# Second attention of a fused graph network: turning x by DMA transposes of f16 halves instead of TensorE transposes

## The reference

```python
q = heads(features @ Wq); k = heads(features @ Wk); v = heads(features @ Wv)      # 8 heads of 32
e = jnp.einsum('whqd,whkd->whqk', q, k)
e = jnp.where(e >= 0, e, ALPHA * e)
attn = jax.nn.softmax(jnp.where(adj[:, None] > 0, e, NEG), axis=-1)
h = jnp.einsum('whqk,whkd->whqd', attn, v)
out = _layernorm(h, g1, b1)
out = jnp.concatenate([out, features], axis=-1) @ Wffn.T
out = _layernorm(out, g2, b2)
return out + features
```

## Time and profile before

| | |
|---|---|
| median of three runs | 3160.52 us (3158.16 to 3162.86) |
| profiled execution, its own time | 3157.04 us |
| its span, first to last instruction | 3155.3 us |
| TensorE busy | 3019.6 us, 96% of the span |
| VectorE, ScalarE, POOL busy | 2482.2, 1999.8, 1672.7 us |
| mean granted TensorE clock | 0.987 of 2.4 GHz |

### The profile page before, as it was taken

One profiled execution on the slowest core, in us unless ns is written; L12 is line 12 of the kernel. 1 busy time (PEld: TensorE's weight loads), 2 busy tenths in 40 slices (PEclk: granted clock), 3 DMA queues, 4 the chain that ended last, 5 costly groups with the idle time before them and its releaser, 6 DMA issues.

```text
span 3155.3 us, 75174 instructions
## 1 busy us (share of the span) xinstructions
PE 3019.6 (96%) x27909; PEld 2049.3 (65%) x27909; DVE 2482.2 (79%) x6757; ACT 1999.8 (63%) x3695; POOL 1672.7 (53%) x1511
## 2 busy tenths in 40 slices
PE   6999999999999976999999998999999999999996
PEld 4666666666666644666666676777777777777773
DVE  5888888888888864666666667888888888888883
ACT  4666656666666644666666656777777777777774
POOL 2555555555554542344444435666666666666665
PEclk9999999999999998999999999999999999999998
DMA  5444444544454423222222224444444444444441
GB/s 163 138 135 140 135 140 131 144 129 145 130 144 131 142 62 92 76 77 78 81 68 81 77 86 142 136 136 147 137 142 140 138 142 135 136 147 137 142 129 41
DMA packets 358327, 382.45 MB, mean 121 GB/s; under 512 B 99264, under 2 KB 266816, under 8 KB 357952
## 3 DMA queue, kind: packets, MB, share of 16 engines
q1 hardware_dynamic: 356800, 376.03, 40.3%
q10 hardware_dynamic: 1152, 1.52, 0.2%
HBM read 242.16 MB, written 118.49 MB: 114 GB/s over the span
## 4 chain that ended last, share of the span: by engine, by line
PE 54%; DVE 2%; DMA 2%; issue 1%; ACT 1%; SPq 1%; POOL 0%; POOLq 0%; DVEq 0%; ACTq 0%
PE bank_heads L2267 4%; PE bank_pair L2146 4%; PE bank_pair L2535 3%; PE bank_pair L2537 3%; PE bank_pair L2536 3%; PE bank_score L2171 3%; PE bank_pair L2149 3%; PE bank_pair L2160 3%; PE bank_proj L2131 2%; PE bank_proj L2133 2%; PE bank_proj L2132 2%; PE bank_back L2131 2%; PE bank_heads L2535 2%; PE bank_heads L2536 2%; PE bank_heads L2537 2%; PE bank_sums L2536 2%
## 5 line engine op out<-in xcount | busy, mean ns | idle before, releaser
L1865 ACT ACTIVATE f_gh<-bank_pair 128x512 f32<-128x512 f32 x512 | 304.3, 594 | 247.3 <-PE bank_pair L2149 247.2
L2488 DVE TENSOR_TENSOR f_gl<-f_act,f_gh 128x512 f16<-128x512 f32 x256 | 281.9, 1101 | 227.1 <-ACT f_act L2416 227.1
L2075 DVE CUSTOM_DVE_ANT_0 b_junk<-bank_score,b_mask 128x256 bf16<-128x256 f32 x1024 | 390.6, 419 | 42.1 <-issue 41.8
L1409 DVE TENSOR_TENSOR a_linked<-a_prob,a_mask 128x1024 f32<-128x1024 f32 x256 | 354.0, 1383 | 3.9 <-ACT a_prob L1206 3.9
L1968 POOL TENSOR_TENSOR f_xb<-f_gh 128x512 f32<-128x512 f32 x256 | 335.6, 1311 | 36.0 <-ACT f_gh L1865 35.7
L2411 ACT ACTIVATE f_gh<-bank_pair,s_f_b 128x512 f16<-128x512 f32 x256 | 175.7, 686 | 252.7 <-PE bank_pair L2537 252.6
L1952 POOL TENSOR_TENSOR b_nw_root<-b_nw_var,b_minus_halves 128x2 f32<-128x2 f32 x128 | 113.0, 883 | 406.8 <-DVE b_nw_neg_mean L2016 406.8
L1206 ACT ACTIVATE a_prob<-a_score_t 128x1024 f32<-128x1024 f32 x256 | 259.5, 1014 | 109.0 <-PE a_score_t L1489 103.0
L1402 DVE TENSOR_REDUCE a_neg_max<-a_score 128x4 f32<-128x1024 f32 x256 | 307.5, 1201 | 2.7 <-PE a_score L1502 2.6
L1871 ACT ACTIVATE bank_pair<-bank_pair 128x512 f32<-128x512 f32 x512 | 305.4, 596 | 0.0
L1447 DVE SCALAR_TENSOR_TENSOR a_qk<-a_proj,a_vcol,a_qk 128x256 f16<-128x256 f32 x256 | 112.1, 480 | 136.6 <-ACT a_qk L1217 136.6
(11 more groups left out here) (275 smaller groups left out, 9748.3 us busy)
## 6 DMA issues: line engine op xcount, KB each, us to landing
a_stack<-qk_scratch SPq DMA_DIRECT2D x384, 128.0 KB, 3.0
qk_scratch<-a_qk SPq DMA_DIRECT2D x64, 512.0 KB, 2.9
qk_scratch<-b_qk SPq DMA_DIRECT2D x64, 512.0 KB, 2.9
first_rows<-qk_scratch SPq DMA_DIRECT2D x192, 128.0 KB, 3.0
f_gl<-qk_scratch SPq DMA_DIRECT2D x192, 128.0 KB, 2.8
a_x_sb<-x_t SPq DMA_DIRECT2D x64, 256.0 KB, 3.3
a_adj_sb<-adj_t SPq DMA_DIRECT2D x64, 256.0 KB, 3.1
a_res<-x_nodes SPq DMA_DIRECT2D x64, 256.0 KB, 3.4
```

Of the source, the lines that this page charges most:

```text
L1409: nc.vector.tensor_tensor(linked[:, k], prob[:, k], mask[:, be[1] % 2].unsqueeze(1).to_broadcast([P, 2, NT * N]), ALU.mult).then_inc(link_ ...
L1865: nc.scalar.activation(prob[:, he], score_t[s].rearrange("p t n -> p (t n)"), ACT.Exp, scale=ALPHA).then_inc(exp_done, 1)
L2075: last = nc.vector.tensor_tensor_reduce(junk[:, s, it], score[s][:, it], mask[:, i, it], -1.0, 3e38, ALU.add, ALU.min, neg_max[:, i, col:c ...
L2488: nc.vector.tensor_tensor(gl[:, bu[1] % 2, f], act32[:, f % 2], gh[:, bu[1] % 2, f], ALU.subtract).then_inc(low_done, 1)
```

## The change

x comes in by nodes, is split by nodes, and the halves are turned by the DMA queue SP. A new buffer `x_nodes` holds both halves by nodes for two graphs. In `AT`, `load` moves from 4 to 0, `xh` from 8 to 6, `xl` from 9 to 7, and a new stage `turn_x` on SP is at 7: the load is issued in slot 0, and six slots later ScalarE splits, VectorE one slot after that. ScalarE's `xh` and VectorE's `xl` now read `x_sb` in SBUF, not the bank. TensorE's `xT` is gone, so bank `proj` is used by `q`, `k` and `v` alone.

```diff
-    AT = {"load": 4, "load_adj": 4, "xT": 8, "xh": 8, "xl": 9, "q": 10, ...
+    AT = {"load": 0, "load_adj": 4, "xh": 6, "xl": 7, "turn_x": 7, "q": 10, ...
+        x_nodes = sb("x_nodes", [P, 2, 2, DC, NT, P], F16)
...
                     if bx := due(t, h, "load"):
                         i = bx[1] % XS
-                        if (n := after(back(bx, XS), 4, 1)) is not None:
-                            sp.wait_ge(proj_done, n)
+                        if (n := after(back(bx, XS), 1, 1)) is not None:
+                            sp.wait_ge(xh_ready, n)
+                            sp.wait_ge(xl_ready, n)
                         sp.dma_start(x_sb[:, i], rows(x_in, bx)).then_inc(x_loaded[i], 16)
+                    if bx := due(t, h, "turn_x"):
+                        i, r = bx[1] % 2, bx[1]
+                        if number(bx) == EARLY:
+                            wait_old(sp, "up_done")
+                        if (n := after(back(bx, XB), 1, 1)) is not None:
+                            sp.wait_ge(out_done, n)
+                        for ready, half, k in ((xh_ready, xh, 0), (xl_ready, xl, 1)):
+                            sp.wait_ge(ready, count(bx, 1, 1))
+                            sp.dma_start_transpose(half[r].rearrange("p c n -> p (c n)").rearrange("p (g n) -> p g n", n=P),
+                                                   x_nodes[:, i, k].rearrange("p c t n -> p (c t n)")).then_inc(x_turned[i], 16)
...
                     if bx := due(t, h, "xh"):
-                        act.wait_ge(proj_done, count(bx, 4, 1))
-                        if number(bx) == EARLY:
-                            wait_old(act, "up_done")
-                        if (n := after(back(bx, XB), 1, 1)) is not None:
-                            act.wait_ge(out_done, n)
-                        nc.scalar.activation(xh[bx[1]], proj[:],
-                                             ACT.Copy).then_inc(xh_ready, 1)
+                        i = bx[1] % 2
+                        act.wait_ge(x_loaded[i], uses(bx, XS) * 16)
+                        if exists(back(bx, 2)):
+                            act.wait_ge(x_turned[i], uses(back(bx, 2), 2) * 32)
+                        nc.scalar.activation(x_nodes[:, i, 0].rearrange("p c t n -> p t c n"),
+                                             x_sb[:, i].rearrange("p t (c n) -> p t c n", c=DC), ACT.Copy).then_inc(xh_ready, 1)
...
                     if bx := due(t, h, "xl"):
-                        r = bx[1]
+                        i = bx[1] % 2
                         dve.wait_ge(xh_ready, count(bx, 1, 1))
-                        nc.vector.tensor_tensor(xl[r], proj[:].rearrange("p (c n) -> p c n", c=DC), xh[r], ALU.subtract).then_inc(xl_ready, 1)
+                        nc.vector.tensor_tensor(x_nodes[:, i, 1].rearrange("p c t n -> p t c n"),
+                                                x_sb[:, i].rearrange("p t (c n) -> p t c n", c=DC),
+                                                x_nodes[:, i, 0].rearrange("p c t n -> p t c n"), ALU.subtract).then_inc(xl_ready, 1)
...
-                    if bx := due(t, h, "xT"):
-                        pe.wait_ge(x_loaded[bx[1] % XS], uses(bx, XS) * 16)
-                        if number(bx) == 0:
-                            wait_old(pe, "row_out")
-                        if (n := after(back(bx, 1), 1, 1)) is not None:
-                            pe.wait_ge(v_ready, n)
-                        for c in range(DC):
-                            for tt in range(NT):
-                                last = nc.tensor.transpose(proj[:, c * N + tt * P:c * N + (tt + 1) * P],
-                                                           x_sb[:, bx[1] % XS, tt, c * P:(c + 1) * P], ident[:])
-                        last.then_inc(proj_done, 1)
                     for j, name in enumerate(("q", "k")):
                         if bp := due(t, h, name):
                             if j == 0:
-                                pe.wait_ge(xl_ready, count(bp, 1, 1))
+                                pe.wait_ge(x_turned[bp[1] % 2], uses(bp, 2) * 32)
+                                if number(bp) == 0:
+                                    wait_old(pe, "row_out")
+                                if (n := after(back(bp, 1), 1, 1)) is not None:
+                                    pe.wait_ge(v_ready, n)
```

More of the change, by code:

```diff
@@ L1613, in attention_second @@
     LATE = 3
-    AT = {"load": 4, "load_adj": 4, "xT": 8, "xh": 8, "xl": 9, "q": 10, "q_hi": 10, "q_lo": 11, "linked": 7, "k": 12, "k_hi": 12, "k_lo": 13,
+    AT = {"load": 0, "load_adj": 4, "xh": 6, "xl": 7, "turn_x": 7, "q": 10, "q_hi": 10, "q_lo": 11, "linked": 7, "k": 12, "k_hi": 12, "k_lo": 13,
           "count": 9, "any": 9, "v": 14, "v_out": 14, "zero_q": 12, "far": 10, "store_qk": 13, "mask": 15, "S": 17, "max": 17,
@@ L1731, in attention_second @@
         proj_done = sem("proj_done")
+        x_turned = [sem(f"x_turned{i}") for i in range(2)]
         xh_ready = sem("xh_ready")
@@ L1911, in slot @@
                             i = bp[1] % 2
-                            act.wait_ge(proj_done, count(bp, 4, j + 2))
+                            act.wait_ge(proj_done, count(bp, 3, j + 1))
                             if j == 0 and exists(back(bp, 2)):
@@ L1916, in slot @@
                     if bx := due(t, h, "xh"):
-                        act.wait_ge(proj_done, count(bx, 4, 1))
-                        if number(bx) == EARLY:
-                            wait_old(act, "up_done")
-                        if (n := after(back(bx, XB), 1, 1)) is not None:
-                            act.wait_ge(out_done, n)
-                        nc.scalar.activation(xh[bx[1]], proj[:],
-                                             ACT.Copy).then_inc(xh_ready, 1)
+                        i = bx[1] % 2
[4 more added lines that the diff above has]
+                                             x_sb[:, i].rearrange("p t (c n) -> p t c n", c=DC), ACT.Copy).then_inc(xh_ready, 1)
                     if bp := due(t, h, "v_out"):
-                        act.wait_ge(proj_done, count(bp, 4, 4))
+                        act.wait_ge(proj_done, count(bp, 3, 3))
                         if number(bp) == EARLY:
```

## The result

The kernel after takes 3167.62 us, the median of eight runs (3165.22 to 3171.74); the kernel before takes 3159.53 us over eight runs (3154.54 to 3162.86). The ratio is 1.0025, with a 95% interval of 1.0015 to 1.0036: 8 us slower. The forecast was 3162 us, range 3142 to 3190, and said that the likeliest was a change within 0.2%.

A forecast was written before the change was run, and what follows sets the result against it. TensorE was taken as the bound, with y on VectorE only 0.20 us from delaying turn_max. Terms +3.5 - 1.5 = +2 us on 3157.04 gave 3159, said as 3162 us for the median of runs; range 3142 to 3190.

The forecast's parts named there:

- `turn_max` and `y`: Slot 1: TensorE's 0.44 us is lost waiting for y; turn_max starts 0.06 us later, +3.5 us over 58 steps.
- The last link: From neg_some through offset and y to turn_max: y ends at 2545.60, turn_max starts 0.08 us later at 2545.68.
- rival 4: VectorE: xl hidden in its waits, y ends as now, turn_max 0.12 us earlier, 3152 us; chance 0.14.
- The first steps: Steps at the start that have no y: may give back up to 1 us more.
- DMA waits: S in slot 1, waiting for a stack in 16 graphs, may come 0.06 us later without cost: some 1 us back.
- Transposes: Two on SP, slot 7: issue 0.62 to 1.23 us each, land before q; cost 0, at most 0.15 us a graph.
- Rival 3: SP: transposes slow throughout, ending 3.4 us after q is due, 197 us over 58 steps, 3358 us; chance 0.02.
- `xh` and `load`: xh moved to slot 6 on ScalarE, hidden behind out_x products; load moved to slot 0; cost 0 for both.
- The sum: Whole kernel: +3.5 - 1.5 = +2 us on the profiled 3157.04 us, so 3159; as median of runs 3162.
- The likeliest case: Whole kernel: the forecast of 3162 us, own range 3154 to 3172, chance 0.50.
- the side that I had given 8 in 100: Whole kernel: the forecast's share of 0.08 for a time more than 0.2% slower.

The follow-up runs named there:

- xl_psum: Kernel after with xl reading a PSUM bank of scores instead of SBUF, comparing instead of subtracting; 3156.26 us, ratio 1.0006.
- xh_last: Kernel after with xh behind v_out on ScalarE, so that xl misses POOL's gap; 3221.65 us, ratio 1.0214.
- after_pad: Kernel after with 72 more already-satisfied waits on TensorE at the program's start; 3160.2 us, ratio 1.0018.
- before_pad: Kernel before with 218 more already-satisfied waits on TensorE at the program's start; 3169.2 us, ratio 1.0043.
- control pair: Both kernels unchanged, one further profile of each; 3156.97 us for the kernel before, 3164.28 us for the kernel after.
- plain_copy: Kernel after with each DMA transpose replaced by a plain DMA of the same bytes, x not turned; 3160.8 us, ratio 1.0024.
- control_after: Kernel after, unchanged, profiled a second time; 3164.28 us.
- xl_early: Kernel after with xh in slot 1, xl in slot 2 behind max, transposes in slot 4; 3180.0 us, ratio 1.0084.
- xl_early2: Kernel after with xh in slot 2, xl in slot 2 behind stats1, transposes in slot 4; 3181.21 us, ratio 1.0072.

## Why the prediction was right, and where its size was off

- **`turn_max` and `y`.** Right: TensorE's 0.44 us a graph is lost whole in a wait for `y`. Counted from the start of `turn_z`, the steps were forecast and measured as: end of `xl` 2.56 and 2.55 us, end of POOL's third affine 3.68 and 3.68, `linked` 3.97 and 3.97, `mask` 5.37 and 5.38, `neg_some` 6.52 and 6.54, `y` 7.42 and 7.35, start of `turn_max` 7.50 and 7.46. `xl_psum` and `xh_last` show the cause from both sides.
- **The last link.** `y` came 0.07 us earlier than forecast. In the kernel before it started at 2544.73, 0.01 us after `offset`, and I took that for its bound; but TensorE's `out` had ended at 2544.42 + 0.27 = 2544.69 (its last matmul), so `y` could have gone 0.04 us earlier at most. In the kernel after `out` ends 0.44 us earlier (2550.08 + 0.27 = 2550.35), and `y` starts 0.08 us before `offset` ends. So the step measured +0.033 us in place of +0.06: 1.8 us over 54 graphs where 3.5 stood in the sum for 58. The same bound makes rival 4 worth more than I gave it: with POOL not held `turn_max` starts at 7.25 us, 0.20 us earlier than before and not 0.12.
- **The first steps, "may give back up to 1 us more".** This is the term that failed. They cost 3.5 us in the profiled pair, and 6.0 to 7.4 us in five other profiles with the split in slots 6 and 7 (77.9 to 79.3 us against a mean of 71.9 for the two profiles of the kernel before). I had asked which waits there would shrink and not what the removed instructions move. The mechanism, in order: fewer TensorE instructions; an instruction packet inside the q/k store of graph 3; the store lands after 4.48 us instead of 2.92; `S`, counted from the start of the store, comes 1.8 us later (1936.20 - 1926.38 against 1932.79 - 1924.77); and 3.4 us more at the lower clock. `after_pad` and `before_pad` show it in both directions.
- **DMA waits, "1 us given back".** Wrong in sign. What goes beyond 54 undisturbed graphs is 6.0 and 5.3 us in the two profiles of the kernel after, 4.3 and 3.6 in those of the kernel before: +1.7 us. The landing of the stack's last block does not explain it: it comes 6.86 against 6.67 us after `turn_z` in the profiled pair (medians of 48 graphs), but 6.61 against 6.62 in the control pair, and 6.63 with plain copies, whose 54 graphs had 5.7 us beyond as well. The traces do show where these waits stand. In both kernels, their controls, the padded kernels and `plain_copy`, the 24 to 29 graphs without an instruction packet from 0.3 us ahead of the start of their q/k store to 8.5 us behind it lose 0.0 to 0.5 us together; the others lose the rest, 3.6 to 4.3 us with `xT` and 4.3 to 6.0 us with the split. Why a packet costs more with the split stays open.
- **Transposes.** That they hide was right: the weight loads of `q` waited for them three times in 64 graphs, 2.0 us in all. Their issue did not halve with their size: it takes 1.26 us, above my upper bound of 1.23. The second lands 8.0 us after `turn_z` instead of the 6.9 to 7.6 forecast, 1.36 us ahead of `q`. Rival 3 fell: the Trainium skill, page "VectorE: DVE Perf Modes", section "The three transpose paths", gives 1309 ns for a 128x128 bf16 tile by DMA, an estimate from that page of 5.2 us for the four tiles of one transpose. The trace does not agree with that product: here four tiles landed 2.9 us after the issue.
- **`xh` and `load`.** Cost 0, as forecast: slots 6 and 7 take 2.633 and 3.292 us in both kernels.
- **The sum.** Forecast +3.5 - 1.5 = +2. Measured by the same terms +1.8, +1.7 and +3.5, together +7.0 of the 8.0 us. The likeliest case had the right mechanism for the steady graph, and its own range (3154 to 3172) held the time, but on the side that I had given 8 in 100. That the whole came out so near was in part luck: the step that the prediction worked out gave 1.8 of the 8.0 us, and the two terms that it took for a gain of 1.5 us cost 5.2 us. In `control_after` the first graphs alone cost twice as much as in this pair.

## What to carry to other kernels

An engine with no idle time gains from work taken off it only as far as the next producer it waits for allows: here 0.20 us of slack, read from two rows, decided over 0.44 us. Before moving an elementwise operation, look at which memory it reads and what POOL does beside it, and then at every chain that runs through that engine's slot, not only at the one to be freed; four kernels here took `y` or `xl` out of the way and lost more through `stats0`, two of them through the queue as well. And where a pipeline starts up with thin buffers, the count of instructions is itself a timing: padding the stream of one engine is a cheap way to see whether a loss in the first steps is the change's own.

## What the runs showed of the hardware

- An instruction packet (16384 bytes, queue 8) that starts 0.75 to 2.35 us behind the start of a 512 KB store makes it late: over the twelve traces without `xl_early` and `xl_early2` there are 32 such stores, and they land after 3.9 to 5.0 us, median 4.4. The 665 stores with no packet from 0.6 us ahead to 2.6 us behind their start land after 2.91 us at the median, 3.8 at most.
- A VectorE operation with both inputs in SBUF that meets a running POOL operation waits for its end: in `xh_last` `xl` started 0.20 us behind POOL's L2004, took 1.61 us instead of 0.68 and ended 0.54 us after it. POOL's next operation is held in turn: in the kernel after L2004 took 1.63 us instead of 1.27, as if it got its inputs 0.14 us before `xl` ended. With one input of `xl` in PSUM neither was held (0.68 and 1.27 us).
- A DMA transpose of 128x512 f16 takes 1.26 us to issue, about as long as one of twice the size (1.23 us); a plain copy of the same bytes takes 0.60 us.
- A wait of TensorE of 2.63 us in the first graphs was followed by 3.4 us at the lower clock level, and one of 2.97 us in `control_after` went with 6.8 us at that level, from 0.8 us before its end. Those of 0.83 to 0.95 us for the same stack in both profiles of the kernel before and in the padded kernels were followed by none.
